# Fused GNN and routed MoE kernel: the last stage of a group dealt out over five tiles instead of four

## The chip, the cores and the metric

The kernel runs on one core of a Trainium2 chip. The metric is the device time of one execution in microseconds (us), median of several runs. All arithmetic named below is fp32 unless said.

## What is computed

For 128 graphs of 128 nodes with 128 features (16,384 rows, "tokens"):

```python
x = x + gnn(layernorm(x), adj)      # adj @ x, @ W1 (128x512), RMS norm, SiLU, @ W2 (512x128)
# second layer, on x after the first
h = layernorm(x)
logits = h @ gate_w + gate_b        # 16 experts
top_v, top_i = top_k(logits, 2); top_w = softmax(top_v)
expert_out[e] = relu(h @ w1[e] + b1[e]) @ w2[e] + b2[e]      # 128 -> 256 -> 128
moe = sum over the two chosen experts of top_w * expert_out
x = x + layernorm(h + moe) * gamma + beta
```

## The kernel before, in words

The 128 graphs are 32 **groups** of four (`NG`, `GB`): 512 tokens each. Three stages follow one another and overlap at their ends.

1. **Groups, first pass.** The graph network, the routing and a scatter: GpSimd writes each group's 1,024 rows (two experts for each token) to the place of its expert in the DRAM tensor `dispatched`.
2. **Tiles.** The rows of an expert are cut into tiles of 256. There are `NT` = 143 tile steps, the most that could be needed; how many hold rows depends on the routing, and the rest compute on rows that nobody reads. For a tile t, SyncE loads the rows and the expert's weights, TensorE transposes (line 670), VectorE copies out (1237), TensorE multiplies by w1 (681), ScalarE does ReLU (841), TensorE multiplies by w2 (691, 696), VectorE scales and adds (`tout`, 1257), SyncE stores the tile to the DRAM tensor `results`. TensorE works one tile ahead of what VectorE writes out.
3. **Last stage of a group.** GpSimd gathers a group's 1,024 rows back from `results` with 8 indirect DMAs of 128 rows (line 534) into one of `RINGM` = 9 buffers. VectorE adds the two rows of each token (`add_up`, 1308), takes the moments (1022), ScalarE takes the root (878) and normalises (870), VectorE multiplies by gamma (1322) and adds (1333), and SyncE writes the group to `out` (454).

Stages 2 and 3 overlap. Every engine runs its own list in order. From tile step `MIX_FROM` = 49 on, `tiles_and_groups` (line 317) writes tiles and last stages into one list for VectorE and ScalarE: **turn** k handles group k (its `add_up`; the later parts of the groups before it), in four pieces, one piece behind each tile. After `MIXED` turns the tiles run without pieces, and the turns that are left follow behind the last tile. SyncE's list is laid out to match (line 459). In the mixed stretch VectorE also computes the return addresses of four groups at a time (`places`, lines 1176 to 1183), behind the tile steps in `PLACES_AT` (52, 64, 76, 88 and 100 are in the mixed stretch); where they go is fixed by the tile step, not by the turn.

GpSimd has a list of gathers alone, group after group. What it waits for:

```python
if g == 0 or g in SEGS or g == ALONE:
    pool.wait_ge(t_out, needs[len([c for c in SEGS if c <= g or g == ALONE])])
...
if g >= RINGM:
    pool.wait_ge(p_n, g - RINGM + 1)
if 1 <= g < ALONE:
    pool.wait_ge(moe_in[(g - 1) % RINGM], ...)
```

The first wait is for tiles: `t_out` counts tiles that VectorE has written out, and `needs` holds, for groups up to some point, how many tiles must be out, plus `LAG` = 3 so that their stores have landed. For the group `ALONE` = `MIXED` + 1 the number is that of all tiles that hold rows, plus 3. The second keeps a gather from overwriting a buffer whose group is not normalised yet. The third, with a wait in the middle of each group (`BURST` = 4), lets at most four gathers be in flight in the groups below `ALONE`; from `ALONE` on there is no such wait. Before, `ALONE` is 24.

Of the kernel before, what the change touches and what calls it, by code (L numbers as in the profile page):

```python
# [6 lines left out]
GB = 4  # L7
# [15 lines left out]
NT = TOK * TOPK // TILE + E - 1  # L23
# [7 lines left out]
NS = len(SEGS) + 2  # L31
LAG = 3
MIX_FROM = max(FIRST + 4 * min(c for c in SEGS if c > g) + E - 1 + LAG - 4 * g for g in range(FULL_AT))
MIXED = (NT - MIX_FROM) // GB
ALONE = MIXED + 1
RINGM = 9
BLANK = 11
# [10 lines left out]
def gnn_moe(nc, x, adj_t, eps, w1, b1, rms_w, w2, b2, gate_w, gate_b, w_exp, w2_exp, b2_exp, gamma, beta, out):  # L48
# [9 lines left out]
    with ctx:  # L58
# [236 lines left out]
        def pipeline(eng, step, first, lead, turns, last, each=RING):  # L295
            for t in range(first, lead):
                step(None, t)
            if turns:
                with eng.Fori(0, turns) as i:
                    for k in range(each):  # L300
                        step(i, lead + k)
            for t in range(lead + turns * each, last):
                step(None, t)
# [13 lines left out]
        def tiles_and_groups(eng, tile_step, post_step, tail_step):  # L317
            pipeline(eng, tile_step, EARLY, EARLY + 1 + RING2, (NG - 1) // RING2 - 1, MIX_FROM, RING2)
            for t in range(MIX_FROM, NT + 1 + LAG):
                tile_step(None, t)  # L320
                turn, quarter = divmod(t - MIX_FROM, GB)
                if turn < MIXED:
                    post_step(turn, (quarter,))
            for turn in range(MIXED, NG - 1):
                post_step(turn)
            tail_step()
# [10 lines left out]
        def _(sp):  # L337
# [58 lines left out]
            def tile_step(i, t):  # L396
                n = t + 4
                loads, keeps = has(i, n, NT), has(i, n - RING2, NT)
                if loads or keeps:
                    got = places_of(table, count(i, n, 1, RING2), 3 if keeps else 2, 0 if loads else 2)  # L400
                    if keeps:
                        sp.wait_ge(t_out, count(i, n - RING2 + 1, 1, RING2))
                        tile_store(n, got[-1], tout[:, n % RING2], t_kept[n % RING2])
                    if loads:
                        tile_load(n, got[0], got[1])
# [45 lines left out]
            def store(g):  # L451
                if 0 <= g < NG:
                    sp.wait_ge(p_o, g + 1)
                    sp.dma_start(out[:, g * GB:(g + 1) * GB, :], o3[:, g % RING]).then_inc(stored[g % RING], 16)
# [3 lines left out]
            pipeline(sp, tile_step, EARLY + RING2 + RING2 // 2 - 4, lead, turns, MIX_FROM, RING2)  # L458
            for t in range(MIX_FROM, NT + RING2 - 4):
                tile_step(None, t)  # L460
                turn, quarter = divmod(t - MIX_FROM, GB)
                if quarter == 3 and turn < MIXED:
                    store(turn - 3)
            for g in range(MIXED - 3, NG):
                store(g)
# [4 lines left out]
        def _(pool):  # L470
# [28 lines left out]
            def step(i, t):  # L499
# [17 lines left out]
            pool.wait_ge(first_kept, 16 * RING2)  # L517
            pool.wait_ge(need_done, 2)
            _, needs = nc.values_load_multi_w_load_instructions(
                need[0:1, :], engines=[mybir.EngineType.Pool], min_val=FIRST, max_val=NT + LAG)  # L520
            for g in range(NG):
# [216 lines left out]
        def _(act):  # L738
# [111 lines left out]
            for t in range(2, 7):  # L850
                tile_step(None, t)
            act.wait_ge(pad_done, 1)
            _, starts = nc.values_load_multi_w_load_instructions(
                pad_row[0:1, E // 2:E], engines=[mybir.EngineType.Activation], min_val=0, max_val=E * CAP)
            for t in range(7, 11):
# [32 lines left out]
            def tail_step():  # L888
                for g in (NG - 2, NG - 1):
# [3 lines left out]
                    normalise(g, 1)  # L893

            tiles_and_groups(act, tile_step, post_step, tail_step)

        @block.vector
        def _(dve):
# [448 lines left out]
            def tail_step():  # L1347
                scale(NG - 2)
                for g in (NG - 3, NG - 2, NG - 1):
# [5 lines left out]
                    finish(g)  # L1355

            tiles_and_groups(dve, tile_step, post_step, tail_step)


# [29 lines left out]
```

## Time and profile before

| | us |
|---|---|
| median of 3 runs | 961.48 |
| lowest and highest | 960.74, 965.85 |
| the profiled execution, its own time | 958.03 |
| its span in the profile | 956.2 |

The profile is of one execution. Its span leaves out 1.8 us of that execution's own time. Times inside it are counted from the start of the span. A busy share averages over stages that differ, so the views below are read for stretches: the mixed stretch runs from about 580 us, when VectorE does its first `add_up`, to about 866 us, when the last tile is out; behind it only the last stage of the groups is left.

### The profile page before, as it was taken

What the parts mean: (1) busy time and instruction counts of PE and PEld (TensorE: products, weight loads), DVE (VectorE), ACT (ScalarE), POOL (GpSimd) and SP (SyncE); (2) the same over time, 40 slices, a digit from 0 to 9 for tenths busy, and PEclk for the clock granted to TensorE, in tenths of its full rate; (3) what the DMA queues carried; (4) which work ended last, traced back from release to release, by engine and by line L of the source; (5) the groups of instructions that cost most, each with busy time, mean ns of one, the idle gap of its engine ahead of it and who ended that gap; (6) DMA issues with size and microseconds to landing.
All of it is one profiled execution on the core that took longest, in us unless ns stands there. A gap on an engine that the chain in (4) does not pass through costs nothing. (4 is left out here: it accounts for less than half of the span.)

```text
span 956.2 us, 15738 instructions
## 1 busy us (share of the span) xinstructions
PE 767.2 (80%) x3649; PEld 504.9 (53%) x3650; DVE 597.2 (62%) x2164; ACT 551.4 (58%) x1123; POOL 506.9 (53%) x539
## 2 busy tenths in 40 slices
PE   5999999999999889848879999999987878872000
PEld 3455555555555445426657777777765656651000
DVE  3678887788778767754746665667655454443223
ACT  3799999999999969762223334454443333332121
POOL 2016666666666656666103555555455555557774
PEclk9999999999999989976989999999998888886555
DMA  5444444444444311142656677777775656653222
GB/s 160 149 176 148 148 150 148 150 150 150 149 150 151 126 49 47 46 110 80 197 144 177 185 190 198 205 210 213 206 212 161 170 154 179 166 145 108 71 82 79
DMA packets 136677, 140.77 MB, mean 147 GB/s; under 512 B 18323, under 2 KB 112291, under 8 KB 136358
## 3 DMA queue, kind: packets, MB, share of 16 engines
q1 hardware_dynamic: 117750, 102.67, 35.8%
q0 software_dynamic: 16384, 34.11, 12.6%
q10 hardware_dynamic: 2480, 3.34, 1.1%
q14 instruction: 47, 0.39, 0.1%
q8 instruction: 16, 0.26, 0.1%
HBM read 74.57 MB, written 65.49 MB: 146 GB/s over the span
## 5 line engine op out<-in xcount | busy, mean ns | idle before, releaser
L510 POOL DMA_INDIRECT dispatched<-rows,slot_i x256 | 250.3, 978 | 204.3 <-issue 129.4
L534 POOL DMA_INDIRECT work<-results,place x184 | 178.8, 972 | 185.4 <-issue 68.6
L841 ACT ACTIVATE hid<-bank,wts 128x256 f32<-128x256 f32 x286 | 120.0, 471 | 269.5 <-PE bank L681 268.0
L681 PE MATMUL bank<-tut,wts 128*128 128x256 f32 x572 | 161.3, 408 | 41.8 <-DVE tut L1237 34.7
L696 PE MATMUL bank<-w_all,hid 128*128 x1144 | 175.2, 299 | 0.0
L1257 DVE SCALAR_TENSOR_TENSOR tout<-bank,gate,tin 128x128 f32<-128x128 f32 x274 | 83.5, 346 | 124.0 <-PE bank L696 116.2
L696 PEld LDWEIGHTS bank<-w_all,hid 128*128 128x128 f32 x1144 | 147.0, 201 | 18.2 <-issue 2.2
L681 PEld LDWEIGHTS bank<-tut,wts 128*128 128x128 f32 x572 | 104.6, 204 | 55.7 <-DVE tut L1237 38.3
L560 PE MATMUL bank<-agg,w_sb 128*128 128x512 f32 x256 | 124.3, 608 | 0.0
L575 PE MATMUL bank<-work,w_sb 128*128 128x512 f32 x256 | 117.9, 604 | 3.8 <-ACT work L826 3.8
L534 POOL DMA_INDIRECT rows<-results,place x72 | 70.9, 985 | 49.5 <-issue 26.7
L1133 DVE SCALAR_TENSOR_TENSOR work<-bank,b_sb,rms_b 128x512 f32<-128x512 f32 x128 | 87.6, 741 | 7.9 <-PE bank L560 7.5
L826 ACT ACTIVATE work<-work,rms_sb 128x512 f32<-128x512 f32 x128 | 84.6, 710 | 0.4
L575 PEld LDWEIGHTS bank<-work,w_sb 128*128 128x128 f32 x256 | 47.6, 192 | 69.1 <-issue 50.1
L785 ACT ACTIVATE rows<-xs,nb,rs 128x256 f32<-128x256 f32 x128 | 66.3, 590 | 25.3 <-DMA dispatched<-rows,slot_i 18.4
L560 PEld LDWEIGHTS bank<-agg,w_sb 128*128 128x128 f32 x256 | 46.8, 193 | 46.9 <-issue 46.9
L670 PE MATMUL bank<-ident,tin 128*128 128x128 f32 x286 | 58.8, 289 | 11.8 <-DMA tin<-dispatched 10.5
L1237 DVE COPY tut<-bank 128x256 f32<-128x256 f32 x143 | 59.3, 415 | 13.2 <-PE bank L670 13.1
L802 ACT ACTIVATE xn<-xs,nb,rs 128x128 f32<-128x128 f32 x128 | 52.4, 484 | 4.7 <-DVE nb L1033 4.7
L1308 DVE TENSOR_TENSOR work<-work 128x512 f32<-128x512 f32 x23 | 16.0, 694 | 62.6 <-DMA work<-results,place 62.6
L1022 DVE BATCH_NORM_STATS2 bn<-xs 128x6 f32<-128x256 f32 x128 | 48.5, 420 | 9.1 <-DMA xs<-in_x 5.7
L626 PE MATMUL bank<-adj_sb,xn 128*128 128x128 f32 x256 | 37.1, 290 | 11.7 <-issue 8.3
(190 smaller groups left out, 1026.0 us busy)
## 6 DMA issues: line engine op xcount, KB each, us to landing
tin<-dispatched SPq DMA_DIRECT2D x143, 132.0 KB, 2.6
wts<-in_w_exp SPq DMA_DIRECT2D x143, 129.0 KB, 2.5
results<-tout SPq DMA_DIRECT2D x26, 704.0 KB, 3.2
results<-tout SPq DMA_DIRECT2D x137, 128.0 KB
xs<-in_x SPq DMA_DIRECT2D x32, 256.0 KB, 2.8
adj_sb<-in_adj_t SPq DMA_DIRECT2D x32, 256.0 KB, 3.1
out<-agg SPq DMA_DIRECT2D x32, 256.0 KB, 2.3
dispatched<-rows,slot_i POOLq DMA_INDIRECT x256, 2.4
```

Of the source, the lines that this page charges most:

```text
L510: nc.gpsimd.indirect_dma_start(dispatched, bass.IndirectOffsetOnAxis(slot_i[:, k, n:n + 1], 0), rows[:, k, n // TOPK, n % TOPK, :], None). ...
L534: nc.gpsimd.indirect_dma_start(moe_of(g)[:, n // TOPK, n % TOPK, :], None, results, bass.IndirectOffsetOnAxis(place[:, g, n:n + 1], 0)).th ...
L560: nc.tensor.matmul(h_ps[c][:, :], w1_sb[:, c * P:(c + 1) * P], agg[:, t % RING], start=True, stop=True).then_inc(h_done, 1)
L575: last = nc.tensor.matmul(out_ps[:, :], w2_sb[:, c, :], work[:, g % RING, c, :], start=(c == 0), stop=(c == HC - 1))
L681: last = nc.tensor.matmul(hid_ps[n % 2][:, c * TILE:(c + 1) * TILE], wts[:, k, c * P:(c + 1) * P], tut[:, n % 2, :], start=True, stop=True)
L696: last = nc.tensor.matmul(exp_ps[n % 2][:, a * D:(a + 1) * D], hid[:, n % 2, c, a * P:(a + 1) * P], w2_all[:, c, bass.ds(e, D)], start=Fal ...
L785: last = nc.scalar.activation(rows[:, k, j, :, 0:D], xs[:, bass.ds(count(i, g, GB) + j, 1), :].broadcast_to([P, TOPK, D]), ACT.Identity, b ...
L826: nc.scalar.activation(z, z, ACT.Silu, scale=rms_sb[:, c:c + 1]).then_inc(s_done, 1)
L841: last = nc.scalar.activation(hid[:, n % 2, c, :], hid_ps[n % 2][:, c * TILE:(c + 1) * TILE], ACT.Relu, bias=wts[:, k, F + c:F + c + 1], s ...
L1133: nc.vector.scalar_tensor_tensor(out=work[:, k, c, :], in0=h_ps[c][:, :], scalar=b1_sb[:, c:c + 1], in1=rms_b[:, k], op0=ALU.add, op1=ALU. ...
L1237: nc.vector.tensor_copy(tut[:, n % 2, :], tut_ps[n % 2][:, 0:TILE]).then_inc(t_ut, 1)
L1257: last = nc.vector.scalar_tensor_tensor(out=into[:, k, a, :], in0=exp_ps[n % 2][:, a * D:(a + 1) * D], scalar=gate[:, n % 2, a:a + 1], in1 ...
```

## The change

`PACE` = 5 takes the place of `GB` = 4 where turns are laid between tiles. A turn is still four pieces behind four tiles, and a fifth tile follows with no piece. The number of turns that fit between step 49 and step 143 falls from 94 // 4 = 23 to 94 // 5 = 18, so `MIXED` is 18 and the turns 18 to 30 (before: 23 to 30) follow behind the last tile. `ALONE`, worked out from `MIXED`, falls from 24 to 19: the gathers of the groups 19 to 23 lose their waits for the gathers before them, and the wait for all tiles stands ahead of group 19 rather than 24. Line numbers after the change are higher by one.

```diff
--- before.py
+++ after.py
@@ -31,7 +31,8 @@
 NS = len(SEGS) + 2
 LAG = 3
 MIX_FROM = max(FIRST + 4 * min(c for c in SEGS if c > g) + E - 1 + LAG - 4 * g for g in range(FULL_AT))
-MIXED = (NT - MIX_FROM) // GB
+PACE = GB + 1
+MIXED = (NT - MIX_FROM) // PACE
 ALONE = MIXED + 1
 RINGM = 9
 BLANK = 11
@@ -318,7 +319,7 @@
             pipeline(eng, tile_step, EARLY, EARLY + 1 + RING2, (NG - 1) // RING2 - 1, MIX_FROM, RING2)
             for t in range(MIX_FROM, NT + 1 + LAG):
                 tile_step(None, t)
-                turn, quarter = divmod(t - MIX_FROM, GB)
+                turn, quarter = divmod(t - MIX_FROM, PACE)
                 if turn < MIXED:
                     post_step(turn, (quarter,))
             for turn in range(MIXED, NG - 1):
@@ -458,7 +459,7 @@
             pipeline(sp, tile_step, EARLY + RING2 + RING2 // 2 - 4, lead, turns, MIX_FROM, RING2)
             for t in range(MIX_FROM, NT + RING2 - 4):
                 tile_step(None, t)
-                turn, quarter = divmod(t - MIX_FROM, GB)
+                turn, quarter = divmod(t - MIX_FROM, PACE)
                 if quarter == 3 and turn < MIXED:
                     store(turn - 3)
             for g in range(MIXED - 3, NG):
```

**GpSimd, around group 19.** Rows of the list before, from the first gather of group 18 on; `moe_in` are the landings of gathers, `p_n` counts normalised groups, `t_out` tiles. A group is four rows.

```order
L534 DMA work<-results,place 128x128 [waits moe_in8,t_out,p_n]
L534 DMA work<-results,place 128x128 x3
L534 DMA work<-results,place 128x128 [waits moe_in0]
L534 DMA work<-results,place 128x128 x3
L534 DMA work<-results,place 128x128 [waits p_n,moe_in0]
L534 DMA work<-results,place 128x128 x3
L534 DMA work<-results,place 128x128 [waits moe_in1]
L534 DMA work<-results,place 128x128 x3
```

And in the changed kernel:

```order
L535 DMA work<-results,place 128x128 [waits moe_in8,t_out,p_n]
L535 DMA work<-results,place 128x128 x3
L535 DMA work<-results,place 128x128 [waits moe_in0]
L535 DMA work<-results,place 128x128 x3
L535 DMA work<-results,place 128x128 [waits t_out,p_n]
L535 DMA work<-results,place 128x128 x7
L535 DMA work<-results,place 128x128 [waits place_done,p_n]
L535 DMA work<-results,place 128x128 x7
```

Group 18 is the same. Group 19 had to wait for the landing of group 18 and, in its middle, for its own first four; now its first gather waits for `t_out` instead, and eight go out in a row, and so for every group behind it.

**VectorE, the end of one turn.** Rows of the list before, from the last piece of turn 14 (the addition, 1333) to the first piece of turn 15; `tut`, `gate` and `tout` rows are one tile.

```order
L1333 TENSOR_TENSOR agg<-xn,xs 128x512 [waits beta_in,p_g,stored0]
L1237 COPY tut<-bank 128x256 [waits t_h,t_tr]
L1241 TENSOR_SCALAR gate<-tin 128x2
L1257 SCALAR_TENSOR_TENSOR tout<-bank,gate,tin 128x128 [waits t_gate,t_o,t_kept3]
L1257 SCALAR_TENSOR_TENSOR tout<-bank,gate,tin 128x128
L1301 SCALAR_TENSOR_TENSOR nb<-bn,rs 128x4 [waits p_rs]
L1308 TENSOR_TENSOR rows<-rows 128x4x128 [waits moe_in6]
```

And in the changed kernel:

```order
L1334 TENSOR_TENSOR agg<-xn,xs 128x512 [waits beta_in,p_g,stored0]
L1238 COPY tut<-bank 128x256 [waits t_h,t_tr]
L1242 TENSOR_SCALAR gate<-tin 128x2
L1258 SCALAR_TENSOR_TENSOR tout<-bank,gate,tin 128x128 [waits t_gate,t_o,t_kept5]
L1258 SCALAR_TENSOR_TENSOR tout<-bank,gate,tin 128x128
L1238 COPY tut<-bank 128x256 [waits t_h,t_tr]
L1242 TENSOR_SCALAR gate<-tin 128x2
L1258 SCALAR_TENSOR_TENSOR tout<-bank,gate,tin 128x128 [waits t_gate,t_o,t_kept0]
L1258 SCALAR_TENSOR_TENSOR tout<-bank,gate,tin 128x128
L1302 SCALAR_TENSOR_TENSOR nb<-bn,rs 128x4 [waits p_rs]
L1309 TENSOR_TENSOR rows<-rows 128x4x128 [waits moe_in6]
```

Between the last piece of a turn and the wait for the next group's gathers (`moe_in6` here) there stood one tile, and now there are two.

## Rows read from the trace of the kernel before

**Rows 1.** The page: span, busy time, and the granted clock in 40 slices.

```profile
span 956.2 us, 15738 instructions
PE 767.2 (80%) x3649; PEld 504.9 (53%) x3650; DVE 597.2 (62%) x2164; ACT 551.4 (58%) x1123; POOL 506.9 (53%) x539
...
PEclk9999999999999989976989999999998888886555
```

**Rows 2.** Busy time, granted clock, DMA share and GB/s in three stretches.

```profile
core 0: us, PE busy (x) PEld busy (x) DVE busy (x) ACT busy (x) POOL busy (x), PEclk, DMA share, GB/s
580.00:694.00 114.00, 107.89 (x667) 83.73 (x665) 79.54 (x257) 55.61 (x140) 58.85 (x60) 1.00 0.77 207
694.00:864.00 170.00, 135.48 (x727) 102.95 (x726) 82.90 (x269) 61.52 (x158) 91.38 (x96) 0.87 0.61 168
864.00:946.00 82.00, 1.79 (x14) 1.36 (x12) 26.76 (x61) 17.23 (x45) 62.50 (x65) 0.52 0.31 90
```

**Rows 3.** Waits of VectorE from 580 to 694: us, times, longest.

```profile
DVE tout L1257 <- PE bank L696: 35.0, 41, 1.7
```

**Rows 4.** Waits of VectorE from 694 to 864.

```profile
DVE work L1308 <- DMA work<-results,place: 29.0, 8, 5.8
DVE rows L1308 <- DMA rows<-results,place: 11.6, 3, 5.7
```

**Rows 5.** Waits of TensorE from 694 to 864.

```profile
PE bank L681 <- DVE tut L1237: 28.7, 11, 5.0
```

**Rows 6.** Timeline of GpSimd: first gathers of groups 0, 12, 13, 24; the last.

```profile
start us, us, engine line op out<-in xcount [idle before <-releaser]
510.83 0.98 POOL L534 DMA_INDIRECT work<-results,place  x1 [48.77 <-DVE tout L1257]
...
693.48 0.94 POOL L534 DMA_INDIRECT work<-results,place  x1 [2.89 <-DMA work<-results,place]
...
708.65 0.94 POOL L534 DMA_INDIRECT work<-results,place  x1 [2.93 <-issue]
...
864.32 0.94 POOL L534 DMA_INDIRECT rows<-results,place  x1 [0.30 <-issue]
...
945.80 0.94 POOL L534 DMA_INDIRECT work<-results,place  x1 [0.30 <-issue]
```

**Rows 7.** Timeline of VectorE (x2: two instructions merged, the time is both).

```profile
509.34 0.61 DVE L1257 SCALAR_TENSOR_TENSOR tout<-bank,gate,tin 128x128 f32<-128x128 f32 x2 [0.83 <-PE bank L696]
...
580.66 0.68 DVE L1308 TENSOR_TENSOR work<-work 128x512 f32<-128x512 f32 x1
...
587.90 0.61 DVE L1257 SCALAR_TENSOR_TENSOR tout<-bank,gate,tin 128x128 f32<-128x128 f32 x2 [1.65 <-PE bank L696]
...
591.32 0.61 DVE L1257 SCALAR_TENSOR_TENSOR tout<-bank,gate,tin 128x128 f32<-128x128 f32 x2
...
617.52 0.61 DVE L1257 SCALAR_TENSOR_TENSOR tout<-bank,gate,tin 128x128 f32<-128x128 f32 x2 [0.77 <-PE bank L696]
...
621.54 0.61 DVE L1257 SCALAR_TENSOR_TENSOR tout<-bank,gate,tin 128x128 f32<-128x128 f32 x2
...
693.33 0.61 DVE L1257 SCALAR_TENSOR_TENSOR tout<-bank,gate,tin 128x128 f32<-128x128 f32 x2 [0.76 <-PE bank L696]
...
693.92 0.69 DVE L1308 TENSOR_TENSOR work<-work 128x512 f32<-128x512 f32 x1
...
695.72 0.61 DVE L1257 SCALAR_TENSOR_TENSOR tout<-bank,gate,tin 128x128 f32<-128x128 f32 x2 [0.69 <-PE bank L696]
...
707.93 0.69 DVE L1308 TENSOR_TENSOR work<-work 128x512 f32<-128x512 f32 x1 [3.25 <-DMA work<-results,place]
...
860.04 0.61 DVE L1257 SCALAR_TENSOR_TENSOR tout<-bank,gate,tin 128x128 f32<-128x128 f32 x2 [0.77 <-PE bank L696]
```

**Rows 8.** Timeline after the last gather, all engines.

```profile
948.40 0.69 DVE L1308 TENSOR_TENSOR work<-work 128x512 f32<-128x512 f32 x1 [4.36 <-DMA work<-results,place]
...
953.03 0.69 DVE L1333 TENSOR_TENSOR agg<-xn,xs 128x512 f32<-128x512 f32 x1
```

## Prediction

> **What bounds the kernel now.** The page [rows 1] has TensorE busy for 80% of the span, more than any other engine. A table of stretches [rows 2] shows three regimes. From 580 to 694 us TensorE is busy for 107.9 of 114 us at a granted clock of 1.00: tiles bound it. From 694 to 864 its busy share falls and the granted clock is 0.86. From 864 on TensorE has nothing left, and GpSimd is busy for 62.5 of 82 us.
>
> The waits say what changes at 694. Up to there VectorE waits for nothing but matmuls [rows 3]. Behind it, in eleven turns (12 to 22), it waits 29.0 + 11.6 = 40.6 us for gathers in front of `add_up` [rows 4], and since its list is in order, the copy of `tut` stands behind that wait and TensorE waits 28.7 us for it [rows 5]. So the tiles there go at the pace of the gathers. The reason is arithmetic. GpSimd's groups start at 510.83 and 693.48, twelve groups apart [rows 6]: 15.22 us a group under the burst waits. VectorE takes its first turn at 580.66 and its twelfth at 693.92 [rows 7]: 10.3 us a turn of four tiles. The turns start 70 us late and gain 4.9 us a group, and at turn 12 (707.93 [rows 7]) they have caught up. From the first gather to the end, the path is thus GpSimd's list: 24 paced groups, then 8 unbroken ones from 864.32 to 945.80 [rows 6], then 10.4 us from the last gather to the end of the span: landing, `add_up` at 948.40, last addition at 953.03 [rows 8], the store.
>
> **The change, part by part.** Two opposite terms, both on that path.
>
> *Tiles no longer wait.* Five tiles a turn take 5 x 2.44 = 12.2 us (2.44 is worked out below) against 15.22 us a gathered group, so VectorE gains only 3.0 us a group. Closest is turn 17, the last one between tiles: it comes at 580.66 + 85 x 2.44 + 7.6 = 795.6 us, and group 17 has landed by about 784 (group 18 would start at 510.83 + 18 x 15.22 = 784.8; group 12 had landed 0.7 us before group 13 started, 707.93 and 708.65 [rows 6, 7]). 11 us to spare, more in every turn before. I expect the regime of 580 to 694 to hold to the last tile.
>
> Its price a tile: turns 0 to 11 hold 44 tiles in 693.92 - 580.66 = 113.3 us [rows 7]. Four address computations (`places`) lie in it. A tile without one takes 695.72 - 693.33 = 2.39 us; with one, 591.32 - 587.90 = 3.42 and 621.54 - 617.52 = 4.02 [rows 7], so 1.03 for the first and 1.63 for each of the other three, 5.9 us. That leaves 107.4 / 44 = **2.44 us a tile**. The bounds are 2.39 (nothing but the tile) and 113.3 / 44 = 2.574 (all of it). I take 2.44, since what is taken off is fixed by the tile step: just one `places` comes after step 93, at 100. The one tile in five without a piece may win a bit of the 0.05 us between 2.39 and 2.44; I count nothing.
>
> *The gate.* Group 19's first gather waits for all tiles that hold rows, plus 3. The routing of these inputs, counted from the reference, fills 137 tiles, so it waits for the 140th of 143. That my count can be trusted shows at the first group: the same count gives 19 + 3 = 22 tiles for group 0, and the 22nd tile's output starts at 509.34, the gather at 510.83 [rows 6, 7], 1.49 us on, the longest idle stretch of GpSimd. The 93rd tile is written at 693.33, so the 140th now comes at 693.33 + 47 x 2.44 + 1.63 = 809.6 us (before: 860.04 [rows 7], 50 us later: 40.6 of waits, the rest tiles that restart at a lower clock). Group 18 has been issued by 800, so GpSimd idles some 11 us, and group 19 starts at 809.6 + 1.49 = **811.1**. Before, unbroken gathers started at 864.32, held by the paced ones and not by the gate (860.04 + 1.49 = 861.5): **53.2 us earlier**.
>
> *Five more groups behind the gate.* Unbroken gathers take (945.80 - 864.32) / 63 = 1.293 us each [rows 6]. Groups 19 to 31 are 104 gathers: 103 x 1.293 = 133.2 us from first to last, 5 x 8 x 1.293 = **51.7 us more** than now. Sum: 811.1 + 133.2 + 10.4 = 954.7 us of span against 956.2, **-1.5 us**.
>
> *What costs nothing, and under what cover.* The last stage of five more groups moves behind the tiles. In that stretch VectorE is busy for 26.8 us and ScalarE for 17.2 in eight groups [rows 2], 3.3 and 2.2 of the 10.3 us that a group's gathers take; gone from the path while gathers are slower than that. The buffers: group 26 is the first whose buffer wait is not met at the gate (group 17 is normalised in turn 18, just behind the last tile at about 817), and its gathers come at 811.1 + 7 x 10.35 = 883.5. SyncE's stores move with their turns; five fewer stand in its list between loads, and each waits for an addition made a turn earlier. TensorE's list is the same. The unbroken gathers now run beside the last three tiles, which hold no rows; if they slow these down, the slack of 66 us before group 26 takes it up.
>
> *A rule weighed.* The row first: 0.86 of the clock from 694 to 864 [rows 2] is the share of time at the lower of two levels, (1 - 0.86) / 0.5 = 28%, and it falls where VectorE holds TensorE up [rows 5]. The Trainium skill (TensorE: Matmul & The Clock Gate, Terms) puts the penalty of a throttled stretch at its length times the missing share of the clock; by it the 170 us would give back 170 x 0.28 x 0.5 = 24 us, where my sum has 50. I go by the waits, since a clock alone does not end them; the rule's figure has a rival of its own, C, worked out there from the rows.
>
> **How this stands to the runs.** The sum is against the profiled execution (span 956.2, its own time 958.03). The median of the runs is 961.48, 3.4 above it; I carry the difference over: 961.48 - 1.5 = **960.0 us**. What a measurement of this kernel can tell from no change is about 0.5%, 4.8 us.
>
> **Rivals.**
>
> - *A, faster: the tiles run at their floor.* With a fifth tile free of pieces all tiles take 2.39. Then the 140th comes at 693.33 - 44 x 0.05 + 47 x 2.39 + 1.63 = 805.1, the end 5.9 us before that of now: 955.6 us. It counts as faster from 2.40 us a tile down. For: the pair of tiles at 2.39 [rows 7]. Against: the 44 tiles average 2.44, and the pieces have only been spread.
> - *B, slower: the clock stays low.* In every stretch behind 694 the granted clock was 0.86. If it is the length of the load and not the waits that brings it down, tiles from the 94th on take 2.44 / 0.86 = 2.84 us, the 140th comes at 693.33 + 47 x 2.84 + 1.63 = 828.3, the end 17.2 us later: 978.7 us. It decides against the change from 2.57 us a tile. For: the clock. Against: it was 1.00 over 114 us of fuller load [rows 2].
> - *C, slower: only the clock's part returns.* The waits for gathers stay (bursts land later beside faster tiles), and what was computed in the 48 us at the lower level (28% of 170) takes 24: the 140th tile comes at 836, the end 25 us later, 986.5 us. The 11 us of slack at turn 17 speak against it.
> - *D, the gate does not hold.* If group 19 went out without waiting, unbroken gathers would start at 510.83 + 19 x 15.22 = 800.0 and end the span at 943.6, 12.6 us earlier: 948.9 us. Group 0's row, released by a tile, speaks against it.
>
> **How the numbers follow.** The forecast, within 0.5%: 0.68. A 0.20, D 0.02: faster 0.22. B 0.08, C 0.02: slower 0.10. The bounds of the tile's price give 955.6 (2.39) and, at 2.574 with all `places` in it, the 140th tile at 814.3 and an end 3.2 us later, 964.7. I widen both by under 1 us for the three runs of before, themselves 5 us apart: 955.0 to 965.5. B, C and D lie outside, 0.12 together.
>
> **What would show it.** Right: VectorE has no wait for gathers before the last tile; granted clock 1.00 from 580 to about 817; the 140th `tout` near 810 and the first gather of group 19 about 1.5 us behind it, after some 11 us idle; then 10.3 us a group to about 944, and 10.4 us to the end. Wrong: waits at `add_up` in turns below 18 (C), tiles over 2.57 us at a lower clock (B), group 19 starting at once behind group 18 (D), or a group's gathers taking other than 10.3 us behind the gate, for which the sum has no room: 0.1 us a group is 1.3 us.

## The result and the profile after

| | before | after |
|---|---|---|
| median of 20 runs, us | 965.1 | 960.17 |
| lowest and highest, us | 955.87, 967.35 | 957.02, 962.06 |
| ratio, with its 95% interval | | 0.9956 (0.9941 to 0.9971) |
| the profiled execution, its span | 958.03, 956.2 | 960.16, 958.3 |

The change makes the kernel 0.44% faster in this measurement, 4.2 us of 965.1 (the medians themselves are 4.9 us apart). The ratio is within the 0.5% that the forecast called no change, though its interval reaches from 0.29% to 0.59%, and the time lies 0.2 us from the forecast one. The two profiled executions say the opposite, spans of 956.2 against 958.3: that of before, 958.03 us by its own time, is not one of the 20 runs, of which all but one took longer, and that of after is at the median of its runs. And the experiments below met chips of another kind: on the two of them on which the changed kernel itself was run, it is 2.7% and 3.3% **slower** than before.

The page of the changed kernel: busy time, and the granted clock in 40 slices.

```profile
span 958.3 us, 15735 instructions
...
PE 750.9 (78%) x3649; PEld 494.0 (52%) x3650; DVE 598.5 (62%) x2164; ACT 552.8 (58%) x1123; POOL 511.9 (53%) x539
...
PEclk9999999999999989986999999999999999655555
```

From the 31st slice on, where the clock of [rows 1] falls to 8, it stays at 9 until the tiles end in the 34th. Stretches of the changed kernel; the columns are those of [rows 2].

```profile
core 0: us, PE busy (x) PEld busy (x) DVE busy (x) ACT busy (x) POOL busy (x), PEclk, DMA share, GB/s
580.00:694.00 114.00, 109.85 (x672) 85.32 (x671) 74.76 (x245) 52.87 (x132) 58.40 (x61) 0.99 0.75 204
694.00:812.00 118.00, 113.22 (x697) 87.59 (x696) 72.59 (x243) 54.32 (x138) 56.47 (x57) 1.00 0.77 209
812.00:948.00 136.00, 5.91 (x37) 4.47 (x36) 42.46 (x98) 28.50 (x73) 103.26 (x104) 0.54 0.30 86
```

TensorE stays busy up to the last tile, at a granted clock of 0.99 and 1.00; in [rows 2] the clock was 0.87 from 694 on. Waits of VectorE from 580 to 812 (us, times, longest):

```profile
DVE tout L1258 <- PE bank L697: 82.4, 85, 2.3
DVE tout L1258 <- issue: 1.4, 1, 1.4
DVE tout L1258 <- DMA results<-tout: 0.7, 1, 0.7
```

There is no wait for a gather: the 40.6 us of [rows 4] are gone. TensorE has a wait in the second stretch, 694 to 812, that it hardly has in the first (0.2 us), for the load of a tile's rows:

```profile
PE bank L671 <- DMA tin<-dispatched: 3.7, 8, 1.0
```

GpSimd's timeline: the first gathers of groups 0 and 18, the last of group 18, the first of group 19, and the last of all, to be held against [rows 6].

```profile
513.52 0.98 POOL L535 DMA_INDIRECT work<-results,place  x1 [50.66 <-DVE tout L1258]
...
793.38 0.94 POOL L535 DMA_INDIRECT work<-results,place  x1 [3.12 <-DVE tout L1258]
...
804.73 0.95 POOL L535 DMA_INDIRECT work<-results,place  x1 [0.30 <-issue]
813.33 0.94 POOL L535 DMA_INDIRECT work<-results,place  x1 [7.66 <-DVE tout L1258]
...
947.86 0.95 POOL L535 DMA_INDIRECT work<-results,place  x1 [0.30 <-issue]
```

VectorE's timeline: `add_up` of turn 0, the 93rd tile, `add_up` of turn 17, and the 140th tile; against [rows 7].

```profile
580.61 0.68 DVE L1309 TENSOR_TENSOR work<-work 128x512 f32<-128x512 f32 x1
...
692.29 0.61 DVE L1258 SCALAR_TENSOR_TENSOR tout<-bank,gate,tin 128x128 f32<-128x128 f32 x2 [0.77 <-PE bank L697]
...
797.83 0.69 DVE L1309 TENSOR_TENSOR rows<-rows 128x512 f32<-128x512 f32 x1
...
811.93 0.61 DVE L1258 SCALAR_TENSOR_TENSOR tout<-bank,gate,tin 128x128 f32<-128x128 f32 x2 [1.37 <-PE bank L697]
```

The 140th tile comes at 811.93 (860.04 before), group 19 at 813.33 after 7.7 us idle, 104 gathers take 134.5 us, and 10.4 us follow. The shape of the stage is the forecast one.

### The profile page after: what moved, and what is told of

Same layout as the page of the kernel before. It is cut to its first block, busy times and chain, and to the rows that moved or that the text cites. A ratio compares the mean times of both kernels' runs of the same rounds, so it can differ in the third digit from the quotient of the medians.

```text
span 958.3 us, 15735 instructions
## 1 busy us (share of the span) xinstructions
PE 750.9 (78%) x3649; PEld 494.0 (52%) x3650; DVE 598.5 (62%) x2164; ACT 552.8 (58%) x1123; POOL 511.9 (53%) x539
## 4 chain that ended last, share of the span: by engine, by line
PE 25%; POOL 23%; SPq 19%; issue 14%; DMA 7%; DVE 6%; ACT 4%; POOLq 0%; ACTq 0%; DVEq 0%
POOL dispatched L511 13%; POOL work L535 8%; SPq L376 7%; PE bank L697 6%; DMA dispatched<-rows,slot_i 5%; PE bank L682 5%; PE bank L576 4%; SPq L394 4%; SPq L387 4%; SPq L389 4%; PE bank L561 4%; POOL rows L535 2%; DVE work L1134 2%; PE bank L633 1%; PE bank L671 1%
## 5 line engine op out<-in xcount | busy, mean ns | idle before, releaser
L535 POOL DMA_INDIRECT work<-results,place x184 | 184.2, 1001 | 178.1 <-DVE tout L1258 64.9
L697 PE MATMUL bank<-w_all,hid 128*128 x1144 | 168.9, 292 | 0.0
L682 PE MATMUL bank<-tut,wts 128*128 128x256 f32 x572 | 152.3, 390 | 8.1 <-DVE tut L1238 5.8
L697 PEld LDWEIGHTS bank<-w_all,hid 128*128 128x128 f32 x1144 | 141.5, 195 | 17.6 <-issue 0.9
L682 PEld LDWEIGHTS bank<-tut,wts 128*128 128x128 f32 x572 | 99.9, 195 | 18.6 <-DVE tut L1238 7.1
L879 ACT ACTIVATE rs<-bn,ln_eps 128x4 f32<-128x4 f32 x32 | 9.4, 293 | 89.2 <-DVE bn L1023 89.2
```

The source lines that it names most:

```text
L535: nc.gpsimd.indirect_dma_start(moe_of(g)[:, n // TOPK, n % TOPK, :], None, results, bass.IndirectOffsetOnAxis(place[:, g, n:n + 1], 0)).th ...
L682: last = nc.tensor.matmul(hid_ps[n % 2][:, c * TILE:(c + 1) * TILE], wts[:, k, c * P:(c + 1) * P], tut[:, n % 2, :], start=True, stop=True)
L697: last = nc.tensor.matmul(exp_ps[n % 2][:, a * D:(a + 1) * D], hid[:, n % 2, c, a * P:(a + 1) * P], w2_all[:, c, bass.ds(e, D)], start=Fal ...
```

## Experiments

The experiments ran in four batches, each on another chip with the kernel before beside it, and before's own median says what kind of chip it was: 988.5 us (e1 to e4), 982.8 (e5 to e8), 966.1 (e9, e10) and 987.0 (e11, e12). Below, a *quick chip* is one where before takes 961 to 966 us, a *slow chip* one where it takes 983 to 988. Ratios are to before on the same chip. Each of these four chips was met in one batch only, so that the kind goes with the chip, and not with the hour, is taken for granted here and not shown.

### e1: the kernel before once more

No edit.

> The kernel before, profiled once more. Theory (its path is GpSimd's list of gathers from the first gather to the end): ratio 1.00, and if this execution is longer than the 956.2 us of the first profile, the time is in the 24 paced groups: about 15.5 us a group in place of 15.2 and 14.4, so that the first unbroken gather starts later than 864.32 by just as much, with the same 82 us from there to the last gather. Rival (before's executions differ at their start): the first gather comes late, not 510.83, by the whole difference, and the paced groups take the same as in the first profile.

Measured, slow chip: 0.9992 (0.9957 to 1.0026), as it must be. GpSimd's timeline: first gather, last of group 23, first of group 24, last of all.

```profile
533.23 0.98 POOL L534 DMA_INDIRECT work<-results,place  x1 [56.94 <-DVE tout L1257]
...
885.87 0.94 POOL L534 DMA_INDIRECT work<-results,place  x1 [0.30 <-issue]
891.36 0.94 POOL L534 DMA_INDIRECT rows<-results,place  x1 [4.55 <-DVE tout L1257]
...
972.90 0.94 POOL L534 DMA_INDIRECT work<-results,place  x1 [0.30 <-issue]
```

The execution is 27.1 us longer than the first profile, and the rival has most of it right: the first gather comes 22.4 us late, and the 24 paced groups take 14.92 us each (533.23 to 891.36), or 14.70 without the last wait, where they took 14.73. What neither theory names is that last wait: ahead of group 24 GpSimd now waits 4.6 us for a **tile**. VectorE never waited for a gather in this execution. Turn 0 comes at 618.6, turn 22 at 882.8: 12.0 us a turn, 3.0 us a tile, where the quick chip of the forecast had 10.3 and 2.57. On this chip before's two lists, tiles and gathers, end together. There is no stall that longer turns could take away.

### e2: five tiles a turn, the bursts and the gate as before

```diff
-ALONE = MIXED + 1
+ALONE = 24
```

> The change with ALONE kept at 24: five tiles a turn, but the groups 19 to 23 are gathered in bursts of four without the wait for all tiles. Theory (the change is a trade on GpSimd's list): group 19 starts at about 798 at once behind group 18, five groups at 14.4 to 15.2 us bring the first unbroken gather to 870 to 874, where the changed kernel has its 24th group at 865.7; so 4 to 8 us slower than the change, 1.00 of the kernel before. Rival (the gain is in the tiles that no longer wait, wherever the gathers stand): as fast as the change, 0.995 to 0.996.

Measured, slow chip: 1.0029 (0.9990 to 1.0069). The ratio is the one that the theory gave, but not for its reason alone: in the profiled executions group 24 starts at 890.56, 0.8 us ahead of e1's, and 11 us are lost behind it (93 us to the last gather, 81.5 in e1), 9 of them in one wait. GpSimd's longest wait from 884 on:

```profile
POOL rows L535 <- ACT adj_sb L871: 9.0, 1, 9.0
```

The 24th group went out beside the last tiles, which then came at 892.1, 905.5 and 914.0; the turns stand behind them, and the gathers of group 26 had to wait for a free buffer. What follows: on a slow chip five-tile turns alone are worth nothing, and gathers in an unbroken row beside tiles cost.

### e3: four tiles a turn, 18 turns

```diff
-PACE = GB + 1
-MIXED = (NT - MIX_FROM) // PACE
+PACE = GB
+MIXED = 18
```

> Four tiles a turn as before, but only 18 turns between tiles, so ALONE is 19 as in the change. Theory (what counts is that the turns do not catch up with the gathers): turns 12 to 17 wait for gathers as before, turn 17 comes at about 780 to 785 behind the 117th tile, the 140th tile at 836 to 841, 25 us later than in the change, and the end as much later: about 985 us, 1.02 of before. Rival (what helps is fewer turns between the tiles and unbroken gathers from group 19 on): as fast as the change, 0.995.

Measured, slow chip: 1.0354 (1.0305 to 1.0402), 1022.0 us. The loss is larger than the expected 1.02, and the mechanism is not there: no turn waits for a gather, since at 3.0 us a tile the turns don't catch up. Group 18 is issued by 815, GpSimd is idle for 60 us, the gate opens at 875.6. With 18 turns of four tiles or of five (e5, e11, on other chips) the loss is much the same; what the three share is `ALONE` = 19.

### e4, e8, e12: no wait for all tiles ahead of group 19

```diff
-                if g == 0 or g in SEGS or g == ALONE:
-                    pool.wait_ge(t_out, needs[len([c for c in SEGS if c <= g or g == ALONE])])
+                if g == 0 or g in SEGS:
+                    pool.wait_ge(t_out, needs[len([c for c in SEGS if c <= g])])
```

> The change without the wait for all tiles ahead of group 19; each group waits for the tiles of its own segment as below it (all of them only ahead of group 29), the groups from 19 on still unbroken. Theory (the gate is what holds the path): group 19 starts at about 798, 15 us earlier than in the change, 13 groups at 10.35 us follow, and the end comes 13 to 15 us earlier: about 946 us, 0.98 of before. Rival (unbroken gathers beside the loads of tiles collide with them): gathers take over 10.35 us a group up to 820 and the last tiles over 2.4 us each, and the gain is under 8 us.

> e4 once more (no wait for all tiles ahead of group 19). If the collision of unbroken gathers with the tiles' transfers belongs to the kernel and not to the chip of the first experiments, tiles stall for 20 to 30 us from group 19 on here too: 0 to 30 us slower than the change run beside it. If it is bound to a chip on which transfers land late, and this one is fast (before at 956 to 967 us), it is 10 to 15 us faster than the change, 0.98 of before.

> e4 a third time (no wait for all tiles ahead of group 19). On a chip where before takes 956 to 970 us: if gathers without pauses stop the tiles' transfers on such a chip too, tiles stall for 20 us and more from group 19 on and it is slower than e11 by 5 to 40 us; if not, group 19 starts at about 809 instead of 813 and it is 0 to 5 us faster than e11.

Measured, all three on slow chips: 1.0379 (1.0323 to 1.0436), 1.0327 (1.0282 to 1.0372), 1.0392 (1.0327 to 1.0458). Beside the changed kernel on the same chip that is 0.5 to 0.6% slower (1.0327 against 1.0274, 1.0392 against 1.0334); the intervals overlap, but both pairs say the same. The theory of e4, 15 us faster, is wrong and its rival right by more than it said. Stretches of e4 before and after group 19 goes out (at 816); columns as above:

```profile
700.00:810.00 110.00, 94.23 (x559) 71.69 (x559) 63.26 (x207) 42.38 (x109) 56.93 (x60) 0.98 0.70 188
816.00:846.00 30.00, 5.76 (x23) 4.00 (x22) 1.71 (x5) 0.84 (x2) 22.67 (x24) 0.59 0.32 84
```

GpSimd issues a gather every 1.25 us, and TensorE is busy for 5.8 of 30 us. In e8 and e12 it is 4.9 and 4.0 of 30. SyncE's issues in e4:

```profile
810.17 0.37 SPq L387 DMA_DIRECT2D tin<-dispatched  x1
810.73 0.35 SPq L389 DMA_DIRECT2D wts<-in_w_exp  x1
...
822.43 0.73 SPq L394 DMA_DIRECT2D results<-tout  x1
825.28 0.69 SPq L387 DMA_DIRECT2D tin<-dispatched  x1
828.77 0.70 SPq L389 DMA_DIRECT2D wts<-in_w_exp  x1
830.16 0.70 SPq L455 DMA_DIRECT2D out<-agg  x1
851.34 0.41 SPq L394 DMA_DIRECT2D results<-tout  x1
```

The load of the weights follows the load of the rows by 0.56 us at 810, and by 3.5 us at 825. The next tile is written only when GpSimd has paused (its last gather goes out at 844.7, then it waits 18 us for a free buffer):

```profile
850.57 0.61 DVE L1258 SCALAR_TENSOR_TENSOR tout<-bank,gate,tin 128x128 f32<-128x128 f32 x2 [26.14 <-remote]
```

It waited 26 us, by its list for the landing of an earlier tile's store ("remote" is an event that no instruction of the profile raised; the other two waits of this row in the list are for engines). The kernels before and after, with bursts of four beside the tiles and the gate ahead of the unbroken gathers, show no such stand. The Trainium skill (DMA: Bandwidth & Descriptors, SWDGE vs HWDGE vs iDMA) has each DMA engine take turns between the queue of GpSimd and that of the other engines. The runs don't bear out an even share: from 816 to 846 the core moved 84 GB/s where it moved 188 before, 24 gathers of 64 KB account for 52 GB/s of them, and the DMA engines were busy for 0.32 of the time. What holds the other transfers back is not shown. On a quick chip this was not tried; e12 was meant for one and met a slow one.

### e6: bursts of eight in the kernel before

```diff
-BURST = 4
+BURST = 8
```

> The kernel before with BURST = 8: eight gathers in flight, one wait a group. If the waits themselves cost and a longer burst harms no one, a group takes 12.9 us instead of 15.2, four-tile turns never catch up, the 140th tile comes at about 812 to 815 and the end 35 to 45 us earlier, ratio 0.96. If it is the number of gathers in flight that holds up the tiles' transfers (as unbroken gathers did in e4), tiles stall for some us behind each burst and the kernel is slower than before: 1.01 to 1.05.

Measured, slow chip: 1.123 (1.1161 to 1.1299). Waits of ScalarE and VectorE for landings, from 600 to 850:

```profile
ACT hid L841 <- remote: 74.8, 11, 8.6
DVE tout L1257 <- remote: 67.9, 15, 7.6
```

A tile costs 3.97 us there (63 in 250 us). Of the two expectations the second holds, with more than twice the loss.

### e7: three gathers in flight, without pauses

```diff
-                if 1 <= g < ALONE:
-                    pool.wait_ge(moe_in[(g - 1) % RINGM], ...)
...
+                    j = g * GB * TOPK + n
+                    if g < ALONE and j >= AHEAD:
+                        pool.wait_ge(flown[(j - AHEAD) % LANES], 16 * ((j - AHEAD) // LANES + 1))
```

with `AHEAD` = 3 and four semaphores `flown` in turn; `add_up` waits for the same four.

> The kernel before with another limit on the gathers below ALONE: each gather waits for the landing of the one three before it, so that at most three are in flight and there is no pause while landings take under 3.75 us. If what holds up the tiles' transfers is how many gathers are in flight, tiles keep 2.4 us, a group takes 10.4 to 11 us, and the end comes 40 us or more earlier: 0.95 to 0.96. If it is that GpSimd issues gathers without a pause, tiles stall as in e4 and the kernel is slower than before, 1.02 or more.

Measured, slow chip: 1.1198 (1.1137 to 1.126). At most three gathers are in flight, fewer than the four of before, and it is 12% slower, as the second expectation said and by more. So it is not their number alone that holds up the tiles' transfers. What before has and e6 and e7 lack is a pause behind every fourth gather; that this pause is what lets the other transfers through fits all of e4, e6 and e7, and was not tried by itself. Neither e6 nor e7 was run on a quick chip.

### e5, e11: the changed kernel again

No edit.

> The changed kernel once more, beside before. Theory (the sign of the change hangs on the pace of the tiles: its end is the 140th tile + 1.5 + 134.5 + 10.4 us, while before's is the later of the gathers' list and the 140th tile + 1.5, + 82 + 10.4): where before takes 956 to 967 us the ratio is 0.995 to 0.997 again; where before takes some 985 us, as in the first four experiments, a tile costs 2.9 us, the 140th comes at about 882, and the change takes 1020 to 1030 us, 1.035 to 1.045 of before. Rival (the change shortens the kernel by the same few us on every chip): 0.995 in either case.

> The changed kernel a third time, beside e12 and before. Theory as in e5: where before takes 956 to 970 us the 140th tile comes at 810 to 813 and the ratio is 0.994 to 0.998; where before takes some 985 us, the 140th at 860 to 880 and the ratio 1.025 to 1.04. Rival: one and the same ratio wherever it runs, which by the two runs so far (0.996 and 1.027) would be between them.

Measured, both on slow chips: 1.0274 (1.0225 to 1.0324) and 1.0334 (1.0275 to 1.0394), with 1010.0 and 1020.0 us. The rival, one ratio for all chips, is out. e11 lies in its expected range, with the 140th tile at 872; e5 lost less than the 1.035 to 1.045 expected, as its 140th tile came at 863.8 and not at 882. GpSimd's timeline in e5: the first and last gather of group 18, the first of group 19, the last of all.

```profile
797.12 0.94 POOL L535 DMA_INDIRECT work<-results,place  x1 [3.75 <-DVE tout L1258]
...
808.41 0.94 POOL L535 DMA_INDIRECT work<-results,place  x1 [0.31 <-issue]
865.18 0.94 POOL L535 DMA_INDIRECT work<-results,place  x1 [55.83 <-DVE tout L1258]
...
998.63 0.94 POOL L535 DMA_INDIRECT work<-results,place  x1 [0.30 <-issue]
```

The gate holds it for 55.8 us, not 7.7; behind the gate all is as on the quick chip, 133.5 us of gathers and 10.3 to the end. What the tiles do while gathers run beside them and once they have stopped, in e5:

```profile
612.00:808.00 196.00, 167.29 (x993) 127.77 (x992) 110.11 (x359) 77.66 (x199) 101.51 (x105) 0.98 0.70 186
812.00:860.00 48.00, 47.69 (x297) 37.08 (x295) 30.46 (x104) 22.75 (x58) 0.00 (x0) 1.00 0.65 176
```

Up to 808, 67 tiles are issued in 196 us, 2.9 us each; from 812 on, with GpSimd idle, tiles take 2.4 us, and TensorE is busy for 47.7 of 48 us. The clock is 0.98 and 1.00, so it is not that; nor is it the turns, which go on as before until 849. VectorE's waits up to 808:

```profile
DVE tout L1258 <- PE bank L697: 41.8, 26, 4.2
DVE tout L1258 <- remote: 26.7, 10, 3.6
DVE tout L1258 <- issue: 9.4, 8, 2.1
```

36.1 us of them are for landings or for nothing that the profile shows; on the quick chip 2.1. SyncE's two loads of a tile stand 0.75 us apart on average up to 808 and 0.56 from 812 on; on the quick chip 0.57 throughout. e11 and e3 show the same turn: 2.94 and 3.03 us a tile from 620 to 808, 2.4 to 2.5 from 818 on.

But not all that a slow chip loses is lost beside gathers. Against the profile of the changed kernel on the quick chip:

| | quick | e5 | later by |
|---|---|---|---|
| last scatter of the first pass | 461.9 | 471.0 | 9.1 |
| first gather | 513.5 | 529.3 | 15.8 |
| 49th tile | 580.1 | 606.8 | 26.7 |
| 140th tile | 811.9 | 863.8 | 51.8 |

9 us are gone by the last scatter, and 7 more in the 52 us in which GpSimd issues nothing (before and e1 show 14 and 8). No experiment looks into these; the ratios are not touched by them, since all kernels are alike up to there.

### e9: tiles with no gather and no turn beside them

```diff
-MIXED = (NT - MIX_FROM) // PACE
-ALONE = MIXED + 1
+MIXED = 0
+ALONE = 0
```

> The changed kernel with no turn between tiles and no gather before all tiles are out (MIXED and ALONE 0), to read the pace of tiles with nothing beside them. Theory (where before takes some 985 us it is the gathers that slow the tiles there, by holding up their transfers): tiles take 2.4 to 2.5 us each from step 49 on here too, the 140th comes at about 830, and the end at 1170 or so, since all 256 gathers follow. Rival (on such a chip the tile's own transfers are slow): 2.8 to 2.9 us a tile also without gathers, the 140th tile beyond 860.

Measured on a quick chip, so that the theory's chip was missed: 1144.5 us. Its 49th and 140th tile:

```profile
579.49 0.61 DVE L1258 SCALAR_TENSOR_TENSOR tout<-bank,gate,tin 128x128 f32<-128x128 f32 x2 [1.51 <-PE bank L697]
...
801.65 0.61 DVE L1258 SCALAR_TENSOR_TENSOR tout<-bank,gate,tin 128x128 f32<-128x128 f32 x2 [1.37 <-PE bank L697]
```

91 tiles in 222.2 us, 2.44 each with the five `places`; the last 30 of them, which have none, take 2.38 (730.15 to 801.65). The changed kernel took 811.93 - 580.1 = 231.8 us for the same tiles, and e10, on e9's chip, 229.3: on a quick chip 18 turns and the gathers beside them cost the tiles 7 to 10 us. On a slow one (e5: 606.8 to 863.8) it is 257 us. Stretch 612 to 800 of e9:

```profile
612.00:800.00 188.00, 184.95 (x1158) 145.10 (x1157) 87.37 (x326) 64.65 (x154) 0.00 (x0) 1.00 0.64 165
```

The core moved 165 GB/s there and 209 beside gathers in the changed kernel, so the tiles' own traffic is not at a limit. That a slow chip's tiles take 2.4 us alone rests on the idle stretches of e3, e5 and e11, not on e9.

### e10: the gate at group 22

```diff
-ALONE = MIXED + 1
+ALONE = 22
```

> The change with ALONE = 22: five tiles a turn, bursts kept up to group 21, the wait for all tiles ahead of group 22. Theory: where before takes some 985 us, GpSimd is no longer idle for 57 us ahead of the wait but for under 15, the 140th tile comes at about 875, and 10 groups at 10.35 us end the kernel at 985 to 990, ratio 1.00 to 1.01, against 1.027 for the change. Where before takes 956 to 967 us: group 22 at about 852, 1.00 of before. Rival (the five-tile turns themselves cost on such a chip): 1.02 or more.

Measured on a quick chip: 0.9981 (0.9962 to 1.0000), where 1.00 was expected. Group 22 starts at 847.0 (852 expected), in the changed kernel at 844.8, and the spans are 960.1 and 958.3. The two are from two measurements, so all that can be said is that on a quick chip the place of the gate moves the end by little, some 2 us. On a slow one this version was not tried; that it would lie between e2 and e5 is a guess.

## Why the prediction was right, and where it was not

**The mechanism and the end points: right.** No wait for gathers in the turns below 18, clock 0.99 to 1.00 up to the last tile, GpSimd idle ahead of the gate (7.7 us, some 11 forecast), the gate open 1.4 us behind the 140th tile (1.49 forecast), 10.4 us to the end. A group behind the gate took 10.45 us (134.5 / 103 x 8) where the sum has 10.35: these are the 1.3 us for which, as the forecast said, it has no room. Term by term, for the profiled execution:

| | forecast | measured |
|---|---|---|
| 140th tile starts | 809.6 | 811.9 |
| first gather of group 19 | 811.1 | 813.3 |
| from it to the last gather | 133.2 | 134.5 |
| last gather to the end | 10.4 | 10.4 |
| span | 954.7 | 958.3 |
| margin of turn 17 over group 17 | 11 | some 5 |

The tile cost 2.466 us (797.83 - 580.6 = 217.2, less 7.6 for `places`, over 85), not 2.44, and not evenly. The 44 tiles up to the 93rd came 1.0 us earlier than the sum has them (692.29 against 693.33); the 47 behind it took 119.6 us (692.29 to 811.93) where the sum has 116.3. That is where the 2.3 us of the 140th tile were lost: a price read where VectorE waited for nothing but matmuls was carried into a stretch in which TensorE waits 3.7 us for the rows of its tiles, about what is missing. On e9's and e10's chip the second stretch too is the dearer one: gathers and turns add 1.5 us to the first 44 tiles and 5.6 us to the last 47. The paced groups took 15.55 us (513.52 to 793.38), not 15.22, which the gate hides.

**The step that was mis-sized: the anchor.** "The sum is against the profiled execution; I carry the difference over." Forecast was -1.5 us against before. The profiles give +2.1, the 20 runs a side -4.2. That the forecast time, 960.0, met 960.17 is luck, since two errors cancel: the changed kernel's span came out 3.6 us longer than the sum, and the 3.4 us carried over from before's profile to its median belong to before, not to after, whose profiled execution (960.16) is its median. Before's runs spread over 11.5 us (6.6 without the lowest) and after's over 5.0. That fits a path through 24 paced groups, each with two waits for landings, against one through tiles that wait for none; but no second profile of before on a quick chip was taken, so that this is where before's 965 comes from is argued, not shown.

**A reading that was off.** The forecast takes the granted clock from 694 to 864 as 0.86; [rows 2] has 0.87. With it the time at the lower level is 26% and not 28%, and the times of B and C move by under 2 us, which changes neither the range nor a chance.

**What the prediction did not see: the tile's price differs from chip to chip.** It took 2.44 us from 44 tiles of one trace and named 2.57 as the pace from which the change is slower. That bound holds. On slow chips a tile beside gathers takes 2.84 us (e5, turns 0 to 13: 191.9 us less 7.6, over 65), the 140th tile comes at 863.8, and the kernel is 2.7 to 3.4% slower. The rival B had the threshold and the sign, and the wrong cause: the granted clock there is 0.98. What slows the tiles, by the waits of e5 and by its stretch without gathers, is that their transfers are issued and land late while gathers run; why they do on these chips and not on the others stays open. C's cause, gathers landing late, is not it either: no turn waits for one.

Worked with the same sum, the change is a trade of one list for another. Before's unbroken gathers start at the later of two ends, that of the paced gathers and the 140th tile, and 92 us follow (81.5 + 10.4). After's start behind the 140th tile alone, and 144 to 145 us follow: five more groups, 52 to 53 us. On the quick chip the start moves from 864.3 to 813.3: 51.0 won, 53.0 paid, +2.1 us between the two profiles. On slow chips before's gathers and tiles end together, at 891.4 in e1; the change starts at 865.2 in e5, since no gather runs beside its last tiles: 26 won, 52 paid, +26 us, as the spans have it (983.3 and 1008.9; e1 and e5 are from two chips, whose medians of before are 6 us apart).

**The part of the change that makes the loss on slow chips** is `ALONE` = 19, not the turns: e2 (turns alone) 1.003, e3 (four-tile turns, `ALONE` = 19) 1.035, on the same chip. `ALONE` sets two things, the gate and the unbroken gathers behind it; taking the gate away alone (e4) does not help, and a gate at 19 with bursts of four behind it was not tried. Which part makes the 0.4% on the quick chip was not tried either.

## What to carry to other kernels

When a change moves the path from one list to another, work out the end of both lists and ask which rows their paces come from; a pace that hangs on how transfers of two queues mix may be another on the next chip, and then the sign of the change is. On three chips of this case, gathers that GpSimd issued one behind the other brought the tiles beside them to a stand (e4, e8, e12): keep a pause between short bursts, and don't set them free before the work beside them is done. And one profiled execution is a poor anchor for 0.5%: before's stood 7 us under the median of its 20 runs.

## What the runs showed of the hardware

- On three of the four chips of the experiments the transfers issued by SyncE are held up while GpSimd issues gathers. Under bursts of four, 0.73 to 0.77 us instead of 0.56 lie between a tile's two loads (e1, e3, e5, e11). Under an unbroken row it is up to 3.5 us, and a tile waits 26 to 32 us (e4, e8, e12). Bursts of eight, or gathers without pauses, cost 12% of the kernel's time on the one of the three where they were tried (e6, e7).
- On the fourth chip, and in the measurement, bursts of four and the turns cost the tiles 7 to 10 us in 230 (e9 against e10 and the changed kernel).
- Behind the tiles, unbroken gathers run at 10.3 to 10.5 us a group on both kinds of chip, beside SyncE's stores of the output.
- The medians of the unchanged kernel lie up to 2.4% apart (965.1 to 988.5), five times the effect measured for the change.
